# Layer-norm statistics taken batch by batch inside two attention stages, in place of two separate passes

## The reference, cut to what matters

```
x = x + tanh(g_xattn[0]) * L0_xattn(layernorm(x), ctx)      # attention, 16 heads of 16, rope
x = x + tanh(g_ffn[0])   * L0_ffn(layernorm(x))             # 8 routed experts (top 2) and a shared one
x = x + tanh(g_xattn[1]) * L1_xattn(layernorm(x), ctx)      # attention, 16 heads of 64, masked
x = x + tanh(g_ffn[1])   * L1_ffn(layernorm(x))             # quantised feed-forward
layernorm(v) = (v - mean(v)) / sqrt(var(v) + 1e-5), over the 256 entries of a token
```

## Time and profile before

| | |
|---|---|
| median of 3 runs | 2200.55 us (2200.15 to 2210.15) |
| the profiled execution | 2206.76 us, span of its trace 2205.0 us |
| `attention0`, first to last residual | 156.6 to 525.3 us |
| `attention1`, first to last residual | 1260.2 to 1988.6 us |
| busy, share of the span | PE 79%, PEld 53%, DVE 66%, ACT 49%, POOL 47% |
| mean granted PE clock | 0.922 of full speed |

### The profile page before, as it was taken

How to read it: one execution, slowest core, us unless ns; L and a number is a source line. 1 busy time by engine, 2 the same in 40 slices (tenths; PEclk the granted TensorE clock), 3 DMA queues, 4 the chain that set the end, 5 groups by cost and what they waited for, 6 DMA issues and landing times. The chain is left out here.

```text
span 2205.0 us, 45979 instructions
## 1 busy us (share of the span) xinstructions
PE 1748.4 (79%) x14366; PEld 1165.7 (53%) x14375; DVE 1445.8 (66%) x2967; ACT 1076.9 (49%) x2519; POOL 1040.6 (47%) x1535
## 2 busy tenths in 40 slices
PE   0588888884278879999967999989989999991366
PEld 0344444442235546666645776767667777771123
DVE  4366666674974334444436777777777787776697
ACT  1266666663532212222213666666666666671464
POOL 1655655530816832323236656666566666540005
PEclk9899999996579989999988999999999999995598
DMA  3000000001810011222113332332222223301002
GB/s 106 11 11 11 10 10 10 10 1 43 252 40 1 1 58 57 74 69 72 59 53 90 82 78 67 78 78 67 67 67 69 67 69 81 78 21 40 0 0 77
DMA packets 89215, 117.59 MB, mean 53 GB/s; under 512 B 16392, under 2 KB 58640, under 8 KB 89104
## 3 DMA queue, kind: packets, MB, share of 16 engines
q1 hardware_dynamic: 76048, 90.08, 15.2%
q0 software_dynamic: 6528, 17.83, 2.9%
q10 hardware_dynamic: 6528, 8.39, 1.1%
HBM read 56.36 MB, written 17.83 MB: 34 GB/s over the span
## 5 line engine op out<-in xcount | busy, mean ns | idle before, releaser
L1060 POOL TENSOR_SCALAR a_P<-a_P,a_RS 128x256 f32<-128x256 f32 x512 | 256.4, 501 | 234.8 <-DVE a_RS L1342 205.5
L1229 ACT ACTIVATE a_P<-a_pS,a_NM 128x256 f32<-128x256 f32 x512 | 238.3, 472 | 199.0 <-DVE a_NM L1338 195.2
L814 DVE TENSOR_REDUCE a_M<-a_pS 128x2 f32<-128x512 f32 x256 | 164.7, 685 | 147.0 <-PE a_pS L625 146.0
L1238 ACT ACTIVATE a_PH<-a_pT 128x512 f16<-128x512 f32 x256 | 154.4, 603 | 79.7 <-PE a_pT L1154 69.3
L1338 DVE TENSOR_REDUCE a_NM<-a_pS 128x2 f32<-128x512 f32 x256 | 174.8, 683 | 26.9 <-PE a_pS L1146 21.4
L1348 DVE TENSOR_TENSOR a_PL<-a_pT,a_PH 128x512 f16<-128x512 f32 x256 | 172.5, 674 | 15.9 <-ACT a_PH L1238 15.9
L753 ACT ACTIVATE a_PT<-a_pT 128x512 f32<-128x512 f32 x256 | 139.1, 598 | 73.3 <-PE a_pT L644 73.1
L1154 PE MATMUL a_pT<-g_ident,a_P 128*128 128x128 f32 x1024 | 155.4, 275 | 21.2 <-POOL a_P L1060 21.2
L1154 PEld LDWEIGHTS a_pT<-g_ident,a_P 128*128 128x128 f32 x1024 | 119.6, 141 | 39.6 <-POOL a_P L1060 20.7
L1930 ACT ACTIVATE me_hh<-me_pH 128x512 f16<-128x512 f32 x72 | 43.0, 597 | 175.5 <-PE me_pH L1917 156.0
L99 PE MATMUL a_pF<-a_ch,xw_XW 128*128 128x256 f16 x512 | 103.0, 285 | 32.3 <-DVE a_VL L1330 29.3
(11 more groups left out here) (427 smaller groups left out, 5250.6 us busy)
## 6 DMA issues: line engine op xcount, KB each, us to landing
a_KD<-a_KN SPq DMA_DIRECT2D x128, 128.0 KB
a_QS<-a_QN SPq DMA_DIRECT2D x128, 128.0 KB
mr_stage<-mw SPq DMA_DIRECT2D x24, 512.0 KB, 4.7
ys<-me_yb SPq DMA_DIRECT2D x72, 128.0 KB
a_ctxin<-ctxT SPq DMA_DIRECT2D x32, 256.0 KB, 2.6
a_KZ<-a_KN SPq DMA_DIRECT2D x64, 128.0 KB
g_X<-x SPq DMA_DIRECT2D x1, 4096.0 KB, 14.7
rows<-mr_row ACTq DMA_DIRECT2D x32, 128.0 KB, 3.6
```

What stands on the lines that cost most here:

```text
L814: nc.vector.reduce_max(M[:, :, a, p2], pS[a][:], AX.X).then_inc(s_max.sem, 1)
L1060: last = nc.gpsimd.tensor_scalar(P32[u % 4][:, a, :], P32[u % 4][:, a, :], RS[u % 4][:, a:a + 1], LIFT, ALU.mult, ALU.mult)
L1229: last = nc.scalar.activation(P32[u % 4][:, a, :], pS[u % 2][:, a, :], ACT.Exp, bias=NM[u % 4][:, a:a + 1], accum_out=SM[u % 4][:, a:a + 1])
L1238: nc.scalar.activation(PH[p2 % 2][:, :, :, j * P:(j + 1) * P].rearrange("p a k q -> p (a k) q"), pT[u % 2][:].rearrange("p a k q -> p (a k ...
```

## The change

The loop over all tiles is taken out of the statistics stages "l1" (behind `attention0`) and "l3" (behind `attention1`). In both attentions DVE gets one more piece of work per batch: it waits for the residual of its batch, and takes the two `bn_stats` of the batch's two tiles into `st`. It stands half a turn behind the residual in `attention0` and one turn behind it in `attention1`. The first statistics stage, "l0", keeps its loop. The table with which routed tokens find their slots is made on the chip before and after alike, and the diff doesn't touch it.

```
-def attention0(nc, ctx, X, mean, rstd, ctxT_d, w_d, bias_d, consts):
+def attention0(nc, ctx, X, st, mean, rstd, ctxT_d, w_d, bias_d, consts):
...
+    measured = s.counter("measured", 1)
...
+                def statistics():
+                    x_done.wait(dve, b, 1)
+                    nc.vector.nop(nofuse=True)
+                    for j in range(2):
+                        last = tile_stats(nc, X, st, 2 * b + j)
+                    last.then_inc(measured.sem, 1)
+
...
-                            *[(t + NEXT, lambda j=j: normalise(j)) for j, t in enumerate(TOKENS)], (WIDTH + 2 * NEXT, low), (OUT + NEXT, residual))
+                            *[(t + NEXT, lambda j=j: normalise(j)) for j, t in enumerate(TOKENS)], (WIDTH + 2 * NEXT, low), (OUT + NEXT, residual), (OUT + 2 * NEXT, statistics))
             batches(dve, work)
-            x_done.wait(dve, B, 0)
+            measured.wait(dve, B, 0)
...
-def attention1(nc, ctx, X, XW, ctxT_d, mask_d, bias_d, consts, POS, GW, y_d):
+def attention1(nc, ctx, X, XW, st, ctxT_d, mask_d, bias_d, consts, POS, GW, y_d):
...
+    measured = s.counter("measured", 1)
...
+                def statistics():
+                    x_done.wait(dve, b, 1)
+                    nc.vector.nop(nofuse=True)
+                    for j in range(2):
+                        last = tile_stats(nc, X, st, 2 * b + j)
+                    last.then_inc(measured.sem, 1)
...
-                            *[(2 * p2 + LAG_PV, lambda p2=p2: out_low(p2)) for p2 in range(PAIRS)], (END, finish))
+                            *[(2 * p2 + LAG_PV, lambda p2=p2: out_low(p2)) for p2 in range(PAIRS)], (END, finish), (END + 1, statistics))
             batches(dve, comb, front, back)
-            x_done.wait(dve, B, 0)
+            measured.wait(dve, B, 0)
...
-            layernorm_stats(nc, c2, "l1", X, st, mean, rstd, whole=True)
+            layernorm_stats(nc, c2, "l1", X, st, mean, rstd)
...
-            layernorm_stats(nc, c2, "l3", X, st, mean, rstd, whole=True)
+            layernorm_stats(nc, c2, "l3", X, st, mean, rstd)
```

More of the change, by code:

```diff
@@ L2423, in network @@
             with ExitStack() as c3:
-                attention0(nc, c3, X, mean, rstd, ctxT_d, w0, b0, roped)
+                attention0(nc, c3, X, st, mean, rstd, ctxT_d, w0, b0, roped)
         end_of_part(nc)
         with ExitStack() as c2:
-            layernorm_stats(nc, c2, "l1", X, st, mean, rstd, whole=True)
+            layernorm_stats(nc, c2, "l1", X, st, mean, rstd)
         with ExitStack() as c2:
@@ L2433, in network @@
             with ExitStack() as c3:
-                attention1(nc, c3, X, XW, ctxT_d, mask_d, b1, consts, POS, GW, scratch[2])
+                attention1(nc, c3, X, XW, st, ctxT_d, mask_d, b1, consts, POS, GW, scratch[2])
             end_of_part(nc)
         with ExitStack() as c2:
-            layernorm_stats(nc, c2, "l3", X, st, mean, rstd, whole=True)
+            layernorm_stats(nc, c2, "l3", X, st, mean, rstd)
         with ExitStack() as c2:
```

## The result

| | before | after |
|---|---|---|
| median (lowest to highest) | 2206.93 us (2199.67 to 2213.85, 10 runs) | 2196.12 us (2181.99 to 2199.11, 10 runs) |
| profiled execution, span of its trace | 2206.76, 2205.0 us | 2192.67, 2191.0 us |
| mean granted PE clock of that execution | 0.922 | 0.917 |

The ratio is 0.9948, with a 95% interval of 0.9928 to 0.9967: about 11 us less. The forecast was 2181.7 us, range 2176 to 2194, so the direction is right, and the measured time lies above the forecast and 2 us above the top of its range. Ten runs put the kernel before itself 6.4 us above the median of three from which the forecast started (2206.93 against 2200.55).

The account below looks back on a forecast made before the run. The prediction took PE to bound the attentions, with DVE's two statistics passes fully on the path at the seams. -21.19 + 1.90 + 0.40 = -18.89 us, carried over to the 2200.55 us median, gave 2181.7 us, range 2176 to 2194.

Parts of the forecast that it names:

- Removed, 21.19 us, and 1.90 at the ends: Both seams lose first statistic to first small operation, 21.19 us; the last batch's statistics and wait add 1.90 us.
- Batches in between, zero: In both attentions, the inner batches' statistics fit DVE's idle gaps (2.40 and 0.83 us) and cost nothing.
- The 0.40 us for batch 14: Last step of attention1: DVE has little idle time, so 0.4 of batch 14's 0.75 us falls on the path.
- Rivals 1 and 3: 1: attention1 statistics delay PE, up to 10.5 us, chance 0.12; 3: both attentions' inner places delay PE, 25.5 us, chance 0.04.
- 0.09 us more per pair: On DVE: by the skill's drain rule, two statistics would take some 0.09 us longer than the trace's 0.33 us pitch gives.
- The base: Whole kernel: the saving is carried from the profiled 2206.76 us over to the median, 2200.55 us, 6.2 us lower.
- PE's clock gives nothing back. Zero, with a few tenths either way.: At the seams: PE's granted clock is already at the 1.2 GHz level before the pass, so its effect is zero.
- move up with everything else: Behind the seams: the next stage's DMAs, issued behind the next barrier, start earlier along with everything else.
- Rival 2: Attention loops: lengthened, shifted DVE code stalls on instruction fetches at loop turns, costing 20.6 us, or 10.3 in attention1 alone; chance 0.06.
- Rival 4: At the seams: they wait for something else, say the table load, so only half is saved, 2191 us; chance 0.02.
- Theory A: From the experiments, whole kernel: the seams are the whole effect, and the difference to 20 us is PE's clock.

Follow-up runs that it names:

- Thrice: The kernel before with each of the two statistics passes behind the attentions made three times in a row; 2252.57 us, ratio 1.0188.
- added: The kernel before with the statistics added in both attentions and both passes over all tiles kept; 2210.38 us, ratio 1.0023.
- gone_dve: The kernel before without both passes, nothing in their place, plus 20 semaphore increments on VectorE behind the small operations of "l1"; 2187.92 us, ratio 0.9895.
- attention1 alone: The kernel before with the statistics moved into attention1 only, the pass behind attention0 staying; 2200.22 us, ratio 0.9971.
- both_act: The whole change plus 48 semaphore increments on ScalarE ahead of its wait in "l1"; 2198.74 us, ratio 0.9948 against the kernel before.
- experiment 4: Extra statistics behind attention1: whole change delayed 1.2 us (2191.85 us) or 2.4 us (2195.6 us), kernel before delayed 2.4 us (2212.07 us).

## Why the prediction was wrong, point by point

- **Removed, 21.19 us, and 1.90 at the ends.** Right in size: 20.06 us less in the seams for 19.29 forecast, the same within 0.1 us in each of the five traces of the whole change. "Thrice" shows that such time is on the path in full.
- **Batches in between, zero.** Right, for both attentions ("added", and `attention1` at 726.7 to 727.4 us in all traces of the change against 727.7 and 727.9). The 0.40 us for batch 14 is too small to be seen. Rivals 1 and 3 fell with this. A remark on the way needs a correction: the section of the Trainium skill that the prediction cites for 0.09 us more per pair (VectorE: DVE Perf Modes, "The DRAIN you can't avoid") also says that a next operation which is not held back for all earlier ones starts earlier, so the 0.33 us pitch does not contradict it. The sum didn't use it.
- **The base.** "The median is 6.2 us lower, 2200.55, and I carry the difference over to it" is the step that failed first: the starting value of the sum was 6 to 7 us too low. Three runs had 2200.15, 2200.55 and 2210.15. Over the four groups of experiments 117 runs of the kernel before have a median of 2207.55 us, and the profiled execution at 2206.76 was the better guide. From 2207 the same sum gives 2188. The prediction's range allowed 2 us for the spread of a median whose three values lay 10 apart.
- **"PE's clock gives nothing back. Zero, with a few tenths either way."** This is the second failed step: a term put at nothing. Pooled, 44 runs of the whole change have a mean of 2194.4 us and 117 of before 2207.6 (standard errors 0.8 and 0.5): 13.3 us less, 6.8 short of the seams. The prediction read the clock around the first seam, where it is 0.5 on both sides. Of the second seam it had no row. The clock there, kernel before, then after:

```profile
1987.88:1990.00 2.12, 0.00 (x0) 0.00 (x0) 0.75 (x1) 0.12 (x1) 0.00 (x0) 0.99 0.00 0
1990.00:2000.81 10.81, 0.00 (x0) 0.00 (x0) 10.56 (x33) 1.16 (x1) 0.00 (x0) 0.50 0.00 0
```

```profile
1975.68:1978.56 2.88, 0.00 (x0) 0.00 (x0) 1.50 (x3) 0.04 (x1) 0.00 (x0) 0.98 0.00 0
```

PE had not "run down before the pass" there: the clock fell 2 us into the seam, and the whole pass ran at the lower level. Nor did the argument ask what the rest of the run gets, though single runs of one kernel, in one group, are 8 to 26 us apart. The clock listed with each run bears on that. At 0.9202 over 2207.6 us the kernel before spends 2 x 0.0798 x 2207.6 = 352 us at the lower level, and some 21 us of it are the passes. Had 20 us of this simply gone, the mean clock would be 0.924. It is 0.9198, and the time at the lower level is again 352 us: some 20 us at 1.2 GHz (standard error 4) have turned up elsewhere. What they cost depends on where they fall. Over whole runs of one kernel, 1 us more at that level goes with 0.16 us more in time, which would make 3 us of them. In stretches where PE sets the pace the traces show more: in `attention0` 3.3 us cost 1.1 us a batch, a third, and the last stage took 6.9 or 9.9 us more for some 28 or 37 us more at the lower level (2 x 0.16 x 50.8 = 16, 2 x 0.38 x 57.7 = 44, 2 x 0.44 x 60.7 = 53), a quarter. At a quarter to a third, 20 us cost 5 to 7 us, the size of what is missing. That they fall in such stretches is not shown.
- **A small part comes back right behind the second seam.** From the first small operation of "l3" to the first `f_HQ`, the seven traces with the whole computation and a second seam of 2.9 us have 154.2 to 154.8 us, the four with one of 12.9 or 14.8 us have 153.4 to 153.9: 0.9 us on average, half of it a longer wait of DVE for the weights' DMA (10.1 against 9.6 us on average). The prediction had the next stage's DMAs "move up with everything else". Why they don't quite is open.
- **What stays open** is why the time at the lower level stays the same. It is not a fixed share of a seam ("thrice": 44.8 measured for 44.5), nor the missing pass ("gone_dve", with a seam total of 21.8 us less, measured 19.8). The last stage is a candidate: with a second seam of 2.9 us and the whole computation it took 57.3 to 60.9 us in seven traces of seven (whole change, "attention1 alone", "both_act"; clock 0.56 to 0.65 in the five of the whole change). But with a long seam it took 50.8, 51.0, 53.2, 57.5, 60.0 and 60.7 us, so a slow one comes without the change too, and experiment 4 did not settle it. Theory A is shown for the seams and the attentions; that the clock takes the rest fits in size and is not shown.
- **Rival 2, fetched code,** had a chance of 0.06 and did not happen here; as a mechanism it is real and was worth 13.9 us in a neighbouring kernel. It was priced at 1.72 us a turn from ACT's stand; on DVE it is 2.8, five times and not six. That ACT's stand is harmless could not be read from that row.
- **Rival 4** is excluded by the traces of the seams.

The range failed for the first two reasons together: 6.4 us of base, and 8 us between the 18.9 forecast and the 10.8 in this measurement (13.3 pooled). The base alone would have shifted the range to about 2182 to 2200, and with no loss to the clock the result would have come out at 2188 even on the right base. Either error alone would have stayed inside the range; the loss is the one in the mechanism.

## What to carry to other kernels

A serial pass between two barriers was worth its whole length in the trace, and can go into any engine gap that is longer than it in each batch; read the gap itself, not the busy share. To see whether work added to a pipeline costs anything, compare single batches at the same granted clock, not the whole stage. Before a forecast of 1%, ask for more than three runs of a kernel whose runs are 10 us apart, and read the clock in each stretch that the change shortens. When an edit changes an instruction count ahead of a long hardware loop, look at the loop turns of the engine that the others wait for: a dozen instructions more or less can cost as much as the edit gains, and instructions that do nothing can bring it back, provided that they reach the stream.

## What the runs showed of the hardware

- A loop of 310 instructions on DVE stood 3.04 to 3.27 us at each turn when it began at instruction 1064, and 0.52 to 0.56 us when it began at 1081 or 1083; the first fetched some 40 KB more at each turn. With both long loops placed well, `attention1` ran through its loop without a fetch.
- No-ops without a wait or a signal are not in the compiled stream; semaphore increments are.
- A batch of `attention0` took 26.2 us at full clock and 27.3 to 27.7 us with 3.3 us at the lower level, in both kernels. At the start of the seam behind `attention1` the granted clock still stood at 0.99 (2.12 us of the kernel before) and 0.98 (2.88 us of the kernel after), although no matmul ran; the 10.81 us that follow in the kernel before have 0.50.
- The last stage, 192 matmuls and the same data, took 50.8 us at a mean granted clock of 0.84 and 60.7 at 0.56, in two executions of one kernel.
- Two statistics directly behind the write of their input start 0.10 us after its end, and one every 0.33 us although a record lasts 0.41.
